# Layer 0's gate and up products as three products of rounded parts, with GpSimd making the rests

## The chip, the cores and the metric

The kernel runs on one core of one Trainium2 chip. The metric is the device time of one execution in microseconds (us). Five engines run their own instruction streams and meet only at semaphores: TensorE (PE; its weight loads are shown apart, as PEld), VectorE (DVE), ScalarE (ACT), GpSimd (POOL) and SyncE (SP, which here only issues transfers). Tiles have 128 partitions; matmul results land in 8 PSUM banks of 512 float32 columns.

## The reference, cut to what matters

Four layers of attention-like and feed-forward blocks run on 1024 tokens of width 256. Only layer 0 matters here. After a layer norm (`xn`) it adds two branches to `x`: a chunked linear attention, and a gated feed-forward whose weights are splines of a few control points.

```
xn = _layernorm(x)
# attention: q, k, v = xn @ w.T in 16 heads; q and k are each a product of two small linear maps
kv = cumsum over chunks of (kc^T vc), shifted by one chunk
o  = qc @ kv + mask(qc @ kc^T) @ vc         # then a norm per head, then o @ wo.T
# feed-forward, 1024 inner channels
gate = xn @ gate_w.T ; up = xn @ up_w.T
x = x + attention + (silu(gate) * up) @ down_w.T
```

A feed-forward of layer 3, far behind, uses weights rounded to three values per group of 64 ("ternary"). Their rounding doesn't depend on any layer, and the kernel does it early, beside layer 0.

## The kernel before

**Layer 0, projection stage.** `xT` holds the normalised input transposed: 2 halves (`k`) by 1024 tokens. ScalarE copies spline results into `V[0]` (gate), `V[1]` (up), `V[2]` (down), 2048 columns each, and VectorE overlays a second spline piece (`second_cubics`, L1274). TensorE projects q and k, then v (L483), then makes the two small linear maps of q and k (L537, 8 steps of two products). For each step ScalarE writes one factor (L974 or L976, into one of two buffers `f2s`) and VectorE multiplies it with the other (L1305). Ahead of its first L1305 VectorE works out the scales of the ternary groups: one long reduction (L1291) and four small tensor_scalar instructions (L1292 to L1295). Behind the last it writes `kpar`, k masked by head parity, in four tensor_scalar instructions of 1024 columns (L1311). TensorE's first score products (L555) wait for them.

**Layer 0, chunk loop.** Eight chunks `c` of 128 tokens. For each, TensorE runs in this order: the scores (L555), gate and up for the first 512 tokens (`gate_up0(c, 0, 0)` and `(c, 0, 1)`, L474), the new key-value product (L589), gate for the other 512 tokens, the product with the accumulated state (L597), the values (L573), and up for the other 512 tokens. In `gate_up0` the chunk number `c` picks 128 of the 1024 inner channels. VectorE masks the four score banks (L1334), multiplies silu(gate) with up (L1328, twice), masks and adds the state (L1341, L1344), and in chunks 0 to 5 does the first part of a ternary step. GpSimd does the rest of it:

```
if c < 6:
    if c:
        dve.wait_ge(tern_ready, c)
    dve.tensor_tensor(by_group(tern_t[0]), tern_part(c), tern_group(2, c), ALU.is_gt)
    dve.tensor_tensor(by_group(tern_t[1]), tern_part(c), tern_group(3, c), ALU.is_lt).then_inc(tern_signs, 1)
```

These are L1349 and L1350. GpSimd waits for `tern_signs`, runs four instructions on 1024 bf16 columns (L1737 to L1740) and increments `tern_ready`. VectorE's next step waits for that. GpSimd also copies v by head parity (`by_parity`, L1729), for `values0`.

**Behind the loop.** TensorE sums squares per head (L604), multiplies the hidden activations with the down weights (L483, 128 instructions), and then with `wo`. VectorE takes four reciprocals (L1359) with a product each (L1360), adds the results to `x`, and normalises for layer 1. GpSimd raises the variances to the power -1/2 (L1714), two instructions per layer.

A product of two float32 operands is issued as two TensorE instructions. Layer 1 already uses `split_product`, in which each operand is a pair of fp32r parts (a rounded one and the rest) and three products are added: hi by hi, hi by rest, rest by hi (L493, L494, L495). There ScalarE makes the rounded part and GpSimd (or VectorE) subtracts.

A PSUM bank is handed on in a fixed rotation (`group`): a product waits until the reader of the bank's last user is done (`reuse`). SP issues all transfers in program order, `lB` (layer 2 and expert gate weights) among the first ones.

Of the kernel before, what the change touches and what calls it, by code (L numbers as in the profile page):

```python
# [80 lines left out]
D_END = D_COL + 6  # L81


def build(nc, dram, out):

    ctx = ExitStack()
    with ctx:
        def sb(name, cols, dt=F32, parts=P):
            return ctx.enter_context(nc.sbuf_tensor(name, [parts, cols], dt))
# [5 lines left out]
        x = sb("x", NT * D)[:, :].rearrange("p (t d) -> p t d", t=NT)  # L95
        xT = sb("xT", KD * T)[:, :].rearrange("p (k t) -> p k t", k=KD)
        const = sb("const", C_COS)[:, :]
        rows = sb("rows", R_END, parts=1)[:, :]
        lB = sb("lB", B_END)[:, :]
# [11 lines left out]
        with nc.sbuf_tensor("arena0", [P, ARENA0], F32) as arena0:  # L111
            pass
        arena = sb("arena", ARENA)
# [109 lines left out]
        eprod_ready, ehid_hi = sem("eprod_ready"), sem("ehid_hi")  # L223
        out_done = sem("out_done")
# [3 lines left out]
        lA = m.cols(A_END + A_END % 2)  # L228
        hid0_at = m.at
        win, phase = m.cols(SPB), m.cols(SPB)  # L230
        hid0 = Carve(arena0, hid0_at).grid(NI, T)
        m.at = hid0_at + NI * T
# [5 lines left out]
        silu0 = Carve(arena0, f2s_at).grid(2, BW)  # L238
        V = [m.cols(SPB) for _ in range(3)]
# [156 lines left out]

        block = ctx.enter_context(nc.Block())
# [3 lines left out]
        def _(sp):  # L401
# [7 lines left out]
            sp.dma_start(lB, dram["lB"]).then_inc(lB_loaded, 16)  # L409
            sp.dma_start(lD, dram["lD"]).then_inc(lD_loaded, 16)  # L410

            sp.wait_ge(x_added, HEAD0["added"])
# [40 lines left out]
        def _(pe):  # L453
# [106 lines left out]
            def gate_up0(c, b, n):  # L560
                wide(g_gu0[c][b][n], lambda k: V[n][:, k * I0 + c * P:k * I0 + (c + 1) * P], xT, b)

# [16 lines left out]
            for c in range(NT):  # L579
                scores0(c)  # L580
                if c == 0:
                    pe.wait_ge(*g_spl[-1][-1][1].ready)
# [18 lines left out]
            for p, g in enumerate(g_sum0):  # L601
                reuse(g)
                pe.wait_ge(osq_ready, 2 * p + 2)
                pe.matmul(g.ps, bdmask, kvbd[:, 2 * p:2 * p + 2, :], start=True, stop=True).then_inc(g.full_sem, 1)  # L604
            pe.wait_ge(*g_gu0[NT - 1][NB - 1][1].ready)
# [318 lines left out]
        def _(act):  # L924
# [304 lines left out]
        def _(dve):  # L1229
# [99 lines left out]

            for c in range(NT):  # L1330
# [25 lines left out]
            for p, g in enumerate(g_sum0):  # L1356
# [350 lines left out]
        def _(pool):  # L1707
# [22 lines left out]

            by_parity(0)
            by_parity(1)
            for n in range(6):
                by_parity(n + 2)
# [6 lines left out]
                pool.wait_ge(tern_ready, n + 1)  # L1741

# [209 lines left out]
```

## Time and profile before

| what | value |
|---|---|
| three timed runs | 795.55 us median (792.79 to 795.62) |
| the profiled execution | 796.97 us, span 795.2 us |
| TensorE busy | 709.8 us (89%) |
| VectorE busy | 561.6 us (71%) |
| ScalarE busy | 370.7 us (47%) |
| GpSimd busy | 347.1 us (44%) |
| mean granted TensorE clock | 0.965 |

A share of the whole span is a mean over stages. The change touches the stretch from 56 to about 191 us, which is layer 0 from the q and k maps to the end of the down product, so that stretch is to be read by itself.

### The profile page before, as it was taken

Reading aid. Unit: us, or ns where it says so; the run is one execution under the profiler, and the core shown is the slowest. Engines: PE = TensorE matmul, PEld = TensorE weight load, DVE = VectorE, ACT = ScalarE, POOL = GpSimd, SP = SyncE. Lnnn points to the kernel's source line nnn. Section 1 sums busy time; section 2 is a strip of 40 time slices with the busy share of each in tenths; the row PEclk is TensorE's granted clock in tenths of the full one; section 3 lists DMA queues with packets and bytes.
Section 4 is the critical chain, followed back from the end, with each engine's and each line's share of the span. In section 5 each row is a group of like instructions: output and inputs, shape, how many; then the busy total and the mean of one; then the engine's idle time right before and its main releaser. Section 6 shows DMA issues by size and latency. Waiting matters only on the chain.

```text
span 795.2 us, 12530 instructions
## 1 busy us (share of the span) xinstructions
PE 709.8 (89%) x4172; PEld 550.7 (69%) x4172; DVE 561.6 (71%) x1096; ACT 370.7 (47%) x782; POOL 347.1 (44%) x260
## 2 busy tenths in 40 slices
PE   3899999998899999999999999998998898865567
PEld 1454555587488989898989899987987346554446
DVE  4256666584599797979797757564776455499995
ACT  2275111201465656565555656564554522575440
POOL 0100589300657474747474848441230110437651
PEclk9999999999999999999999999999999899978798
DMA  9400000000401010100101010001110000100001
GB/s 306 201 1 2 1 1 2 1 1 2 151 21 34 8 39 5 28 25 20 33 20 33 20 33 20 21 7 41 40 40 0 1 0 1 33 1 0 0 1 53
DMA packets 11328, 24.76 MB, mean 31 GB/s; under 512 B 1217, under 2 KB 5538, under 8 KB 10786
## 3 DMA queue, kind: packets, MB, share of 16 engines
q1 hardware_dynamic: 10928, 23.19, 8.8%
q10 hardware_dynamic: 370, 1.18, 0.5%
q8 instruction: 18, 0.29, 0.2%
q14 instruction: 12, 0.10, 0.0%
HBM read 23.31 MB, written 1.05 MB: 31 GB/s over the span
## 4 chain that ended last, share of the span: by engine, by line
PE 58%; DVE 24%; issue 7%; POOL 6%; ACT 3%; DMA 2%; DVEq 1%; SPq 0%; POOLq 0%; ACTq 0%
PE bank L493 9%; PE bank L495 8%; PE bank L494 8%; PE bank L483 7%; PE bank L474 7%; PE bank L659 4%; PE bank L689 3%; PE bank L688 2%; DVE x L1426 2%; PE bank L673 2%; DVE zone L1603 2%; PE bank L537 2%; DVE arena L1400 2%; DVE arena L1401 2%; DVE arena L1410 2%
## 5 line engine op out<-in xcount | busy, mean ns | idle before, releaser
L493 PE MATMUL bank<-zone 128*128 128x256 f32 (+1 forms) x520 | 180.5, 347 | 9.0 <-DVE arena L1401 4.0
L495 PE MATMUL bank<-zone 128*128 128x256 f32 (+1 forms) x520 | 169.9, 327 | 0.0
L494 PE MATMUL bank<-zone 128*128 128x256 f32 (+1 forms) x520 | 169.6, 326 | 0.0
L1751 POOL TENSOR_TENSOR arena<-arena 128x512 f32<-128x512 f32 x64 | 82.1, 1282 | 84.5 <-ACT arena L1044 75.7
L493 PEld LDWEIGHTS bank<-zone 128*128 128x128 f32 x520 | 99.4, 191 | 26.2 <-DVE arena L1401 9.5
L495 PEld LDWEIGHTS bank<-zone 128*128 128x128 f32 x520 | 99.3, 191 | 8.7
L494 PEld LDWEIGHTS bank<-zone 128*128 128x128 f32 x520 | 99.7, 192 | 6.6
L1756 POOL TENSOR_TENSOR arena<-arena 128x512 f32<-128x512 f32 x64 | 82.4, 1287 | 32.3 <-DVE arena L1401 23.0
L1745 POOL TENSOR_TENSOR zone<-arena,zone 128x512 fp32r<-128x512 f32 (+1 forms) x56 | 58.6, 1058 | 60.6 <-ACT zone L1106 47.7
L474 PE MATMUL bank<-xT,arena 128*128 128x512 f32 x160 | 77.2, 621 | 2.0 <-ACT xT L935 0.8
L1063 ACT ACTIVATE arena<-arena 128x256 f32<-128x256 f32 (+1 forms) x128 | 62.1, 487 | 32.0 <-DVE arena L1410 31.9
L1426 DVE SCALAR_TENSOR_TENSOR x<-bank,arena,x 128x256 f32<-128x256 f32 x128 | 53.0, 471 | 15.0 <-PE bank L495 14.7
L1410 DVE CUSTOM_DVE_ANT_0 arena<-bank,const 128x256 f32<-128x256 f32 (+1 forms) x128 | 46.2, 403 | 24.6 <-PE bank L659 24.4
L1714 POOL TENSOR_TENSOR lnw<-lnw,minus_half 128x4 f32<-128x4 f32 x8 | 8.1, 1015 | 125.1 <-DVE lnw L1248 125.1
L879 PE MATMUL bank<-zone 128*128 128x512 f32 x128 | 38.3, 455 | 25.4 <-DVE arena L1613 22.5
L659 PE MATMUL bank<-arena 128*128 128x256 f32 (+1 forms) x256 | 59.8, 366 | 0.0
L1400 DVE TENSOR_TENSOR arena<-bank,arena 64x512 f32<-64x512 f32 x64 | 44.4, 693 | 16.2 <-ACT arena L1044 14.7
L474 PEld LDWEIGHTS bank<-xT,arena 128*128 128x128 f32 x160 | 29.3, 195 | 33.4 <-issue 30.4
L879 PEld LDWEIGHTS bank<-zone 128*128 128x128 f32 x128 | 27.8, 225 | 34.8 <-DVE arena L1613 24.6
L689 PE MATMUL bank<-arena 128*128 128x128 f32 x256 | 49.5, 275 | 0.7 <-ACT arena L1031 0.7
L1044 ACT ACTIVATE arena<-bank 128x512 f32<-128x512 f32 x64 | 37.5, 586 | 24.6 <-PE bank L495 24.6
L659 PEld LDWEIGHTS bank<-arena 128*128 128x128 f32 x256 | 43.5, 190 | 4.5
(266 smaller groups left out, 1407.0 us busy)
## 6 DMA issues: line engine op xcount, KB each, us to landing
arena<-in_qk SPq DMA_DIRECT2D x16, 256.0 KB, 2.8
arena<-in_tern SPq DMA_DIRECT2D x1, 3072.0 KB, 22.0
arena<-in_wv SPq DMA_DIRECT2D x8, 256.0 KB, 2.8
arena<-in_wo SPq DMA_DIRECT2D x16, 128.0 KB, 2.1
arena<-in_w SPq DMA_DIRECT2D x8, 256.0 KB, 2.7
lB<-in_lB SPq DMA_DIRECT2D x1, 1288.5 KB, 24.5
arena<-in_lA SPq DMA_DIRECT2D x1, 1282.5 KB, 15.3
x<-in_x SPq DMA_DIRECT2D x1, 1024.0 KB, 12.9
```

The lines of the kernel that those rows point to most:

```text
L474: last = pe.matmul(g.ps, weight(k), act[:, k, b * BW:(b + 1) * BW], start=(k == 0), stop=(k == KD - 1))
L493: pe.matmul(dst, lhi, rhi, start=(n == 0), stop=False)
L494: pe.matmul(dst, lhi, rlo, start=False, stop=False)
L495: last = pe.matmul(dst, llo, rhi, start=False, stop=(n == len(terms) - 1 and not open_end))
L659: last = pe.matmul(ps[2 + g % 2][:, tt * 2 * P + lo:(tt + 1) * 2 * P], qT1[:, tok(t)], kT1[:, t * P - P + lo:t * P + P], start=True, stop= ...
L689: last = pe.matmul(ps[6 + g // 2][:, tok(t % TPB)], v1[:, t, mine], pT1[:, t, 1, :], start=(t == 0), stop=True)
L879: last = pe.matmul(g.ps, weight, part[:, k, b * BW:(b + 1) * BW], start=(k == 0 and m == 0), stop=(k == KD - 1 and m == 1))
L1063: last = act.activation(S1[:, t, lo:], S1[:, t, lo:], ACT.Exp, scale=-1.0, bias=nmax[:, t:t + 1], accum_out=rsum[:, t:t + 1])
L1410: last = dve.tensor_tensor_reduce(S1[:, t, lo:], ps[2 + g % 2][:, tt * 2 * P + lo:(tt + 1) * 2 * P], winmask[:, lo:], -SC1, 3.0e38, ALU.ad ...
L1426: last = dve.scalar_tensor_tensor(out=x[:, t, :], in0=ps[bank][:, tt * D:(tt + 1) * D], scalar=rinv[:, t:t + 1], in1=x[:, t, :], op0=ALU.m ...
L1751: pool.tensor_tensor(qraw[:, j, :], qraw[:, j, :], cosT[:, at], ALU.mult).then_inc(cos_done, 1)
L1756: pool.tensor_tensor((kT1, qT1)[j % 2][:, at], qraw[:, j, :], qsin[:, j, :], ALU.add).then_inc(qk_ready, 1)
```

## The change

Gate and up of layer 0 become `split_product`s. For that each operand gets two fp32r parts.

- `xT`: ScalarE writes rounded copies (four instructions of 512 columns) into memory in which `lB` lies otherwise. GpSimd subtracts them from `xT` and writes the rests over `xT` in place (four instructions).
- Weights: ScalarE writes rounded copies of `V[0]` and `V[1]` (`round_gu`, eight instructions of 512 columns) into `gu_part`, one ahead of each step's `f2s` instruction. GpSimd writes the rests over `V[0]` and `V[1]` (`rest_of_gu`, eight instructions), four of them ahead of the first two `by_parity` copies and four behind.
- TensorE waits for `xT0_split` and `gu_split` ahead of chunk 0 and for the last rests ahead of chunk 4.
- The ternary steps go to chunks 0, 2, 4 and 6, and the last two into VectorE's loop over the norm, behind its second and fourth pass.
- The load of `lB` moves behind the last gate and up product; `lD` moves up one place.

```diff
             def gate_up0(c, b, n):
-                wide(g_gu0[c][b][n], lambda k: V[n][:, k * I0 + c * P:k * I0 + (c + 1) * P], xT, b)
+                g, at = g_gu0[c][b][n], slice(b * BW, (b + 1) * BW)
+                reuse(g)
+                split_product(g.ps, [(parts([gu_part[:, c, (n * KD + k) * P:(n * KD + k + 1) * P], Vr[n][:, k * I0 + c * P:k * I0 + (c + 1) * P]]),
+                                      cut(parts(xT0), ALL, k, at)) for k in range(KD)]).then_inc(g.full_sem, 1)
...
                 if c == 0:
-                    pe.wait_ge(*g_spl[-1][-1][1].ready)
+                    pe.wait_ge(xT0_split, KD * NB)
+                if c % 4 == 0:
+                    pe.wait_ge(gu_split, 4 + c)
...
+            for k in range(KD):
+                for b in range(NB):
+                    at = slice(b * BW, (b + 1) * BW)
+                    act.activation(xT0[0][:, k, at].bitcast(F32R), xT[:, k, at], ACT.Copy).then_inc(xT0_hi, 1)
+
+            def round_gu(cc, n):
+
+                k, h = divmod(cc, 2)
+                act.wait_ge(*g_spl[cc][n][1].ready)
+                act.activation(gu_part[:, 4 * h:4 * h + 4, (n * KD + k) * P:(n * KD + k + 1) * P].bitcast(F32R),
+                               V[n][:, cc * BW:(cc + 1) * BW].rearrange("p (c i) -> p c i", c=4), ACT.Copy).then_inc(gu_hi, 1)
+
             for mm in range(4):
                 for b in range(NB):
                     n = mm * NB + b
+                    round_gu(GU_ORDER[n // 2], n % 2)
...
-                if c < 6:
-                    if c:
-                        dve.wait_ge(tern_ready, c)
-                    dve.tensor_tensor(by_group(tern_t[0]), tern_part(c), tern_group(2, c), ALU.is_gt)
-                    dve.tensor_tensor(by_group(tern_t[1]), tern_part(c), tern_group(3, c), ALU.is_lt).then_inc(tern_signs, 1)
+                if c % 2 == 0:
+                    ternary_signs(c // 2)
...
+                if p % 2:
+                    ternary_signs(4 + p // 2)
...
+            pool.wait_ge(*g_v0[-1].full)
+            for n in range(KD * NB):
+                k, b = divmod(n, NB)
+                at = slice(b * BW, (b + 1) * BW)
+                pool.wait_ge(xT0_hi, n + 1)
+                pool.tensor_tensor(xT0[1][:, k, at].bitcast(F32R), xT[:, k, at], xT0[0][:, k, at], ALU.subtract).then_inc(xT0_split, 1)
+            for n in range(4):
+                rest_of_gu(n)
             by_parity(0)
             by_parity(1)
+            for n in range(4, 8):
+                rest_of_gu(n)
             for n in range(6):
-                by_parity(n + 2)
+                if n < 3:
+                    by_parity(2 * n + 2)
...
+                if n < 3:
+                    by_parity(2 * n + 3)
...
             sp.dma_start(raw3, dram["tern"]).then_inc(raw_loaded, 16)
+            sp.dma_start(lD, dram["lD"]).then_inc(lD_loaded, 16)
+
+            sp.wait_ge(*g_gu0[NT - 1][NB - 1][1].full)
             sp.dma_start(lB, dram["lB"]).then_inc(lB_loaded, 16)
-            sp.dma_start(lD, dram["lD"]).then_inc(lD_loaded, 16)
```

## Rows read from the trace of the kernel before

**Rows 1.** Engines' busy time by stretch: us, PE, PEld, DVE, ACT, POOL, PEclk, DMA share, GB/s.

```profile
84.00:94.50 10.50, 10.50 (x104) 5.91 (x96) 7.40 (x12) 1.86 (x4) 7.87 (x4) 1.00 0.01 2
```

**Rows 2.** PE in order of time, chunk loop: start us, us, instructions, [idle before <-releaser].

```profile
83.20 1.17 PE L555 MATMUL bank<-arena 32*128 32x128 f32 x32
...
88.29 1.88 PE L474 MATMUL bank<-xT,arena 128*128 128x512 f32 x4
90.01 0.61 PE L597 MATMUL bank<-arena 128*128 128x128 f32 x4
...
93.48 1.17 PE L555 MATMUL bank<-arena 32*128 32x128 f32 x32
...
146.14 1.17 PE L555 MATMUL bank<-arena 32*128 32x128 f32 x32
```

**Rows 3.** The chain that ended last, one ternary step: start us, us, what.

```profile
105.28 1.23 DVE arena L1349
...
116.06 1.23 DVE arena L1349
```

**Rows 4.** PE in order of time, experts of layer 1, fp32r products of 512 columns.

```profile
546.05 0.39 PE L493 MATMUL bank<-zone 128*128 128x512 f32 x1
...
553.76 0.39 PE L494 MATMUL bank<-zone 128*128 128x512 f32 x1
```

**Rows 5.** DVE in order of time, beside an idle and beside a busy POOL.

```profile
79.27 0.43 DVE L1344 TENSOR_TENSOR arena<-arena 128x256 f32<-128x256 f32 x1
...
89.63 1.11 DVE L1344 TENSOR_TENSOR arena<-arena 128x256 f32<-128x256 f32 x1
...
691.85 3.00 DVE L1627 TENSOR_SCALAR arena<-arena,small 128x1024 f32<-128x1024 f32 x1 [8.29 <-ACT arena L1164]
694.88 4.31 DVE L1628 TENSOR_TENSOR_SCAN arena<-arena 128x1024 f32<-128x1024 f32 x1
699.12 0.66 DVE L1619 TENSOR_SCALAR arena<-arena 128x1024 f32<-128x1024 f32 x1
```

**Rows 6.** POOL in order of time, at the moment of the DVE row at 691.85.

```profile
691.89 5.16 POOL L1812 TENSOR_TENSOR arena<-arena 128x1024 f32<-128x1024 f32 x2 [6.06 <-ACT arena L1164]
```

**Rows 7.** All engines in order of time, projection stage.

```profile
55.76 13.91 PE L537 MATMUL bank<-arena 128*128 128x512 f32 x32
...
55.96 0.60 ACT L964 ACTIVATE arena<-bank 128x512 f32<-128x512 f32 x1 [1.13 <-PE bank L483]
...
59.44 0.21 DVE L1292 TENSOR_SCALAR tern_s<-tern_s 128x96 bf16<-128x96 f32 x1
...
60.48 1.41 DVE L1305 SCALAR_TENSOR_TENSOR arena<-bank,arena 128x512 f32<-128x512 f32 x2 [0.22 <-DVE tern_s L1295]
...
70.49 2.74 DVE L1311 TENSOR_SCALAR arena<-arena,const 128x1024 f32<-128x1024 f32 x4
...
73.37 1.17 PE L555 MATMUL bank<-arena 32*128 32x128 f32 x32 [0.90 <-DVE arena L1311]
```

**Rows 8.** Groups by line and shape, 0 to 260 us: busy us, mean ns, idle before.

```profile
L1745 POOL TENSOR_TENSOR zone<-arena,zone 128x512 fp32r<-128x512 f32 x6 | 7.8, 1306 | 5.4 <-DMA arena<-in_cossin 5.3
L1334 DVE TENSOR_TENSOR arena<-bank,const 128x512 f32<-128x512 f32 x32 | 19.8, 679 | 1.0 <-PE bank L555 1.0
L1050 ACT ACTIVATE zone<-arena 128x512 fp32r<-128x512 f32 x4 | 2.5, 634 | 1.6 <-DMA arena<-in_qk 1.6
```

**Rows 9.** Behind the loop: PE, DVE and POOL in order of time.

```profile
155.87 3.60 PE L604 MATMUL bank<-arena,const 128*128 128x512 f32 x8
...
171.15 3.35 DVE L1359 RECIPROCAL arena<-arena 128x512 f32<-128x512 f32 x1
...
193.01 1.02 POOL L1714 TENSOR_TENSOR lnw<-lnw,minus_half 128x4 f32<-128x4 f32 x1 [44.63 <-DVE lnw L1248]
```

**Rows 10.** Transfers by tile: issues, KB each, median us to landing.

```profile
arena<-in_lA SPq DMA_DIRECT2D x1, 1282.5 KB, 15.3
```

**Rows 11.** Engines' busy time by stretch, columns as in the first group.

```profile
542.00:544.00 2.00, 2.00 (x5) 1.61 (x6) 0.00 (x0) 0.00 (x0) 0.04 (x1) 0.50 0.76 220
```

More of the change, by code:

```diff
@@ L81 @@
 D_END = D_COL + 6
+LA_COLS = -(-A_END // 16) * 16
+GU_HI = LA_COLS + (NI // 2) * T
+GU_LO = LA_COLS + NI * T + 2 * P + SPB // 2
 def build(nc, dram, out):
@@ L95, in build @@
         x = sb("x", NT * D)[:, :].rearrange("p (t d) -> p t d", t=NT)
+        with nc.sbuf_tensor("rounded_x", [P, 2 * KD * T], F32) as rounded_x:
+            rounded_x = rounded_x[:, :]
         xT = sb("xT", KD * T)[:, :].rearrange("p (k t) -> p k t", k=KD)
+        lB = sb("lB", B_END)[:, :]
         const = sb("const", C_COS)[:, :]
         rows = sb("rows", R_END, parts=1)[:, :]
-        lB = sb("lB", B_END)[:, :]
         lD = sb("lD", D_END)[:, :]
@@ L112, in build @@
             pass
+        with nc.sbuf_tensor("below_hi", [P, GU_HI], F32):
+            with nc.sbuf_tensor("gu_hi0", [P, NI * 4 * P], F32) as gu_hi0:
+                pass
+        with nc.sbuf_tensor("below_lo", [P, GU_LO], F32):
+            with nc.sbuf_tensor("gu_lo0", [P, 2 * SPB], F32) as gu_lo0:
+                pass
         arena = sb("arena", ARENA)
@@ L223, in build @@
         eprod_ready, ehid_hi = sem("eprod_ready"), sem("ehid_hi")
+        xT0_hi, xT0_split, gu_hi, gu_split = sem("xT0_hi"), sem("xT0_split"), sem("gu_hi"), sem("gu_split")
         out_done = sem("out_done")
         m = Carve(arena0)
-        lA = m.cols(A_END + A_END % 2)
+        lA = m.cols(LA_COLS)
         hid0_at = m.at
@@ L231, in build @@
         hid0 = Carve(arena0, hid0_at).grid(NI, T)
+        gu_part = Carve(gu_hi0).grid(NI, 4 * P)
+        xT0 = [rounded_x.rearrange("p (a k t) -> p a k t", a=2, k=KD)[:, 1 - a] for a in range(2)]
         m.at = hid0_at + NI * T
@@ L238, in build @@
         silu0 = Carve(arena0, f2s_at).grid(2, BW)
+        assert m.at == GU_LO and hid0_at + (NI // 2) * T == GU_HI
+        Vr = [Carve(gu_lo0, n * SPB).cols(SPB) for n in range(2)]
         V = [m.cols(SPB) for _ in range(3)]
@@ L395, in build @@
         g_down3 = [group(x_added, b) for b in SUMS]
+        GU_ORDER = (0, 2, 1, 3)
         block = ctx.enter_context(nc.Block())
@@ L604, in _ @@
                 pe.matmul(g.ps, bdmask, kvbd[:, 2 * p:2 * p + 2, :], start=True, stop=True).then_inc(g.full_sem, 1)
+            pe.wait_ge(*g_spl[-1][-1][1].ready)
             pe.wait_ge(*g_gu0[NT - 1][NB - 1][1].ready)
@@ L1328, in hidden0, with ternary_signs @@
                 dve.tensor_tensor(hid0[:, c, b * BW:(b + 1) * BW], g.ps, silu0[:, (c * NB + b) % 2, :], ALU.mult).then_inc(g.ready_sem, 1)
+            def ternary_signs(n):
+                if n:
+                    dve.wait_ge(tern_ready, n)
+                dve.tensor_tensor(by_group(tern_t[0]), tern_part(n), tern_group(2, n), ALU.is_gt)
+                dve.tensor_tensor(by_group(tern_t[1]), tern_part(n), tern_group(3, n), ALU.is_lt).then_inc(tern_signs, 1)
             for c in range(NT):
@@ L1729, in by_parity, with rest_of_gu @@
                 pool.tensor_copy(own, v0[:, c, :].rearrange("p (g r e) -> p r g e", r=2, e=DK0)).then_inc(vpar_ready, 1)
+            def rest_of_gu(at_n):
+                cc, n = GU_ORDER[at_n // 2], at_n % 2
+                k, h = divmod(cc, 2)
+                pool.wait_ge(gu_hi, at_n + 1)
+                whole = V[n][:, cc * BW:(cc + 1) * BW].rearrange("p (c i) -> p c i", c=4)
+                rest = Vr[n][:, cc * BW:(cc + 1) * BW].rearrange("p (c i) -> p c i", c=4)
+                pool.tensor_tensor(rest.bitcast(F32R), whole, gu_part[:, 4 * h:4 * h + 4, (n * KD + k) * P:(n * KD + k + 1) * P],
+                                   ALU.subtract).then_inc(gu_split, 1)
+            pool.wait_ge(*g_v0[-1].full)
[6 more added lines that the diff above has]
+                rest_of_gu(n)
             by_parity(0)
             by_parity(1)
+            for n in range(4, 8):
+                rest_of_gu(n)
             for n in range(6):
-                by_parity(n + 2)
+                if n < 3:
+                    by_parity(2 * n + 2)
                 w, (t0, t1) = tern_part(n), [by_group(t) for t in tern_t]
```

## The prediction

> **What bounds the kernel now.** I read the page first: TensorE is busy 89% of the span and carries 58% of the chain that ended last. Then the stretches, to see whether that holds where the change sits. In the chunk loop TensorE is busy 10.50 of 10.50 us at a granted clock of 1.00, VectorE 7.40, GpSimd 7.87 [rows 1]. Then TensorE in order of time. The scores of one chunk start at 83.20 and of the next at 93.48, so an unhindered chunk takes 10.28 us. From 83.20 to 146.14 there are six chunks, 62.94 us, where six of 10.28 would be 61.68. So 1.26 us of the loop is waiting [rows 2]. The chain shows for what: a ternary step goes round VectorE and GpSimd in 10.78 us (105.28 to 116.06), a little slower than TensorE's 10.28 [rows 3]. So two limits lie close together in the loop, TensorE's work first and the ternary round second, and the change loosens both. The reader should not take the chain's many GpSimd pieces there as the price of the ternary steps: removing them alone is worth 1.3 us.
>
> **TensorE's gain.** Gate and up take 16 instructions per chunk, at one start every 0.43 us: four of them fill 88.29 to 90.01, which is 1.72 us [rows 2]. That is 6.88 us. After it they are 2 (gate, up) by 2 (halves of the tokens) by 2 (`k`) by 3 products, 24 instructions. The same helper with the same shape starts 34 instructions in the 7.71 us from 546.05 to 553.76, one every 0.227 us [rows 4]: 24 take 5.44 us. The difference is 1.44 us per chunk, 11.5 us for eight. The bounds: the 24 can't be faster than these rows, and at the worst the switches between float32 and fp32r products cost 0.1 us each, four a chunk, which leaves 8.3 us. I take 11.5, since nothing but the order of neighbours differs.
>
> **The ternary round.** One step per two chunks, so one round of 10.78 us against two chunks of 10.28 - 1.44 = 8.84 us each. The 1.3 us of waiting go. Sum of gains: 12.8 us.
>
> In a chunk that follows a ternary step VectorE starts the score masks later. Counted from that chunk's first score product: product for L1328 ends 0.8, two comparisons of 1.23 us end 3.3, four masks of about 0.6 end 3.9 to 5.8 [rows 3, 8]. TensorE needs the first mask's bank for the third gate/up group, at 1.1 (scores) + 2.7 + 0.5 = 4.3 us, and the fourth mask at about 6.2, for the values. Both are in time by 0.4 us. If VectorE were late by more, it would delay four chunks by the excess.
>
> **What ScalarE adds.** Twelve copies of 512 columns, 0.63 us each [rows 8]. Four come behind its v copy of 55.96, so they end near 58.7 [rows 7]. The eight others go one to a step, and a step takes TensorE 13.91 / 8 = 1.74 us while ScalarE then needs 0.63 + 0.65. It catches up. Cover: TensorE's own 13.9 us. Without that cover 7.6 us would show. I take nothing.
>
> **What GpSimd adds, and whom it blocks.** Twelve subtractions of 512 columns at 1.31 us [rows 8], 15.7 us in all, from about 57.2 on, in a stretch where GpSimd did next to nothing before. They are needed by chunk 0 (eight of them, ready near 68 to 69) and chunk 4, so by themselves they delay nobody. But they meet VectorE. At 691.85 VectorE's tensor_scalar on SBUF and a pair of GpSimd subtractions start together; the tensor_scalar takes 3.00 us where the same form takes 0.66 at 699.12, and the next VectorE instruction takes 4.31 us [rows 5, 6]. Read as turns: one GpSimd instruction, one of VectorE, the second of GpSimd, the second of VectorE. The addition with both inputs in SBUF does the same on a smaller scale: 0.43 us beside an idle GpSimd, 1.11 us beside a ternary step [rows 5]. The masks with one input in PSUM hold 0.68 us in the mean over all 32, most of them beside a busy GpSimd [rows 8], so such instructions don't wait.
>
> In the projection stage two groups of VectorE are of the first kind. (a) The four small L1292 to L1295, at 59.44 [rows 7]: each waits up to one subtraction of 1.31 us. Three are chained, so GpSimd takes its turn between them. That puts L1295's end near 64.3 where the first L1305 began at 60.48, about 3.8 us late. TensorE can be four steps ahead; its second product of step 4 wants its bank at about 63.6 and gets it at 65.2. From there on ScalarE and VectorE pace the stage: ScalarE needs about 1.2 us a step with its new copy, and the last L1305 ends about 2.3 us later than before. (b) `kpar`, four instructions in 2.74 us at 70.49 [rows 7]. By then GpSimd has one or two subtractions left, shifted by the same turns: each costs one turn, 1.4 us in total by my placing of them. TensorE waits for `kpar` directly (L555 at 73.37 is idle before it until L1311) [rows 7]. Together 3.7 us. The low end is 0.5 us (the small ones don't queue, GpSimd is through before 70.5); the high end is eight turns less the 2.5 us that (a) has in hand, 8 x 1.31 - 2.5 = 8.0 us. I take 3.7, since the row at 691.85 shows turns and the slack is read from rows.
>
> The Trainium skill ("SBUF — State Buffer", section "Who interferes with whom") says that a VectorE instruction in a two-port mode, tensor_scalar among the candidates, and a GpSimd instruction exclude each other for the whole of an instruction, and that one with at most one SBUF input outside these modes never meets GpSimd. The row at 691.85 agrees with the exclusion. The Trainium skill's page also says that whoever starts first goes first, where the row shows VectorE started 0.04 us earlier and still lost the turn; by the order of the Trainium skill's page the sum would change by less than one turn, 1.3 us. By the same page of the Trainium skill the L1305 and the reduction L1291 stay as they are; no row here shows the reduction beside GpSimd.
>
> **What is moved.** `lB`'s load is issued at the end of the loop and needed 40 us later, behind down, `wo` and the norm; `lA`, as large, landed in 15.3 us behind other loads [rows 10]. SP's next wait is behind down and `wo` as well, so nothing queued behind it starts later. Cost nothing; it would cost one for one past 40 us. `lD` has no waiting reader in either place. The `by_parity` copies: `by_parity` 3, 5 and 7 now follow a ternary step that ends at least a chunk before the values need them. No cost.
>
> Behind the loop VectorE gets two more pairs of comparisons. Counted from the loop's end (155.87 before): norm passes 0 and 1 end at 11, comparisons at 14, passes 2 and 3 at 22 to 24 (their second instructions have two SBUF inputs and may wait one turn each), comparisons at 27, against the last reciprocal's end at 18.6 before [rows 9]. The fourth down product comes at about 31, so the adds are in time by some 3 us. GpSimd's last step ends near 34, and the power for the norm came 37.1 us behind the loop's end [rows 9]. It is free by about 3 us. No cost, but the cover is thin.
>
> **Sum.** 12.8 - 3.7 = 9.1 us. The profiled execution took 796.97 us (span 795.2), so 787.9 in its terms. It is 1.4 us above the median of the runs shown, 795.55, which gives 786.5 us.
>
> **The rivals.**
> Forecast: both gains come, VectorE and GpSimd take turns as above, 784.5 to 789. Chance 0.55.
> Rival 1, no turns in the projection stage: the small instructions don't queue and GpSimd is through by `kpar`. Loss 0.5 us, time 783.3, 782.5 to 784.5. For it: GpSimd's position at 70.5 is my placing. Against it: the row at 691.85. Chance 0.18.
> Rival 2, more of it: TensorE idles for several microseconds ahead of chunk 0 and its clock falls. At 542 to 544 the granted clock was 0.50 after a thin stretch [rows 11]; some 4 us at that level cost 2 us. Or the turns reach 8.0 us. Or a late mask costs some tenths in four chunks. 788.5 to 791.5. Chance 0.15.
> Rival 3, the tail: the last ternary step holds GpSimd when the norm of layer 1 wants it. 3 us of slack, then one for one. If the two norm passes and the step itself lose 8 us instead of the 3 I counted, the time is 791.5: no measurable change. Chance 0.06.
> Rival 4, slower: every VectorE instruction of the projection stage waits for GpSimd, L1305 too. Then all of GpSimd's new work, 15.7 us and two copies of 0.4, lies on the path, less the slack of 2.5: 14.0 us against 12.8, time 796.8. It is slower by over 0.5% from a delay of 16.8 us on, so turns that also stretch GpSimd's own instructions by a fifth decide it, at 799.6. Against it: the masks' 0.68 us. Chance 0.06.
>
> Rival 1 and the forecast hold 0.73, rival 2 brings it to 0.88. The range goes from 783 to 791. About 0.5%, 4 us, is what a measurement of this kernel can tell from no change: faster means below 791.6, slower above 799.5. Chances: faster 0.85, within 0.10, slower 0.05.
>
> **What would show it.** Starts of two neighbouring score groups 8.8 to 8.9 us apart. L493 to L495 in the loop one start every 0.227 us, no idle before them by L1334. L1292 to L1295 spread over more than 3 us; L1311 lasting 4 us or more; the first scores of the loop at 77 instead of 73.4; then the loop's end near 147. L1714 of layer 1 with idle time before it, released by VectorE. The prediction is wrong if the chunks take 9.3 us or more (a VectorE wait), if the first scores come past 82, or if L1714 waits for GpSimd's own L1740.

## The result, and the profile after

| | before | after |
|---|---|---|
| median of five runs each | 795.62 us (792.79 to 796.63) | 787.28 us (786.71 to 788.79) |
| profiled execution | 796.97 us, span 795.2 | 786.71 us, span 784.9 |
| ratio of the times, 95% interval | | 0.9902 (0.9881 to 0.9923) |

Faster by 8.3 us in the medians, 10.3 us between the two profiled executions. The forecast was a gain of 9.1 us to 786.5 us, range 783 to 791. The total came out; two of its three terms were too large and their errors largely cancelled. So the parts are the interesting thing. Line numbers moved with the edit: each new number is named beside its old one where it matters.

The stretch of the chunk loop that [rows 1] showed before, and the whole of the unhindered loop, by engine (columns as in [rows 1]):

```profile
84.00:94.50 10.50, 10.50 (x131) 8.47 (x124) 8.53 (x13) 1.85 (x4) 7.49 (x4) 1.00 0.01 2
76.00:146.00 70.00, 70.00 (x740) 55.74 (x733) 46.00 (x69) 17.50 (x35) 32.75 (x21) 1.00 0.01 1
```

TensorE is busy in all 70.00 us at a granted clock of 1.00. Nothing else holds the loop any more: VectorE has 24 us to spare and GpSimd 37. The same stretch in order of time, TensorE (L574 was L555, the scores; L512 to L514 are the three products of rounded parts; L628 was L604, down):

```profile
55.52 7.89 PE L556 MATMUL bank<-arena 128*128 128x512 f32 x18
64.10 6.28 PE L556 MATMUL bank<-arena 128*128 128x512 f32 x14 [0.69 <-DVE arena L1343]
...
75.09 1.17 PE L574 MATMUL bank<-arena 32*128 32x128 f32 x32 [1.90 <-DVE arena L1349]
...
83.63 1.17 PE L574 MATMUL bank<-arena 32*128 32x128 f32 x32
...
91.03 0.50 PE L512 MATMUL bank<-rounded_x,gu_hi 128*128 128x512 f32 x1
91.37 0.39 PE L513 MATMUL bank<-rounded_x,gu_hi 128*128 128x512 f32 x1
...
137.55 1.17 PE L574 MATMUL bank<-arena 32*128 32x128 f32 x32
...
146.00 3.59 PE L628 MATMUL bank<-arena,const 128*128 128x512 f32 x8
```

Three readings. The loop, from the first scores to down, takes 146.00 - 75.09 = 70.91 us, where before it took 82.50 (73.37 to 155.87) [rows 7, 9]: 11.59 us gained, 12.8 forecast. From 83.63 to 137.55 six chunks take 8.99 us each, with no idle time shown; 8.84 was forecast. Within a run the products start every 0.233 us, but the first of a run costs 0.34 (91.03 to 91.37). And the first scores start 19.57 us behind the first product of the q and k maps (L556, was L537); before it was 73.37 - 55.76 = 17.61 [rows 7]. So the start of the loop lost 1.96 us, where 3.7 was forecast. 11.59 - 1.96, and 0.24 us by which the projection stage happened to start earlier, are the 9.87 us between 155.87 and 146.00.

VectorE in the projection stage (L1330 to L1333 were L1292 to L1295, L1343 was L1305, L1349 was L1311):

```profile
59.21 0.38 DVE L1330 TENSOR_SCALAR tern_s<-tern_s 128x96 bf16<-128x96 f32 x1
59.62 1.20 DVE L1331 TENSOR_SCALAR tern_s<-tern_s 128x96 f32<-128x96 bf16 x1
60.85 1.19 DVE L1332 TENSOR_SCALAR tern_s<-tern_s 128x96 f32<-128x96 f32 x1
61.96 1.30 DVE L1333 TENSOR_SCALAR tern_s<-tern_s 128x96 f32<-128x96 f32 x1
63.30 1.41 DVE L1343 SCALAR_TENSOR_TENSOR arena<-bank,arena 128x512 f32<-128x512 f32 x2
...
70.42 0.75 DVE L1343 SCALAR_TENSOR_TENSOR arena<-bank,arena 128x512 f32<-128x512 f32 x1 [0.34 <-PE bank L556]
71.21 3.83 DVE L1349 TENSOR_SCALAR arena<-arena,const 128x1024 f32<-128x1024 f32 x4
```

GpSimd in the same stretch (L1790 makes the rests of `xn`, L1782 those of the weights):

```profile
57.01 4.97 POOL L1790 TENSOR_TENSOR rounded_x<-xT,rounded_x 128x512 fp32r<-128x512 f32 x4 [30.66 <-ACT rounded_x L994]
61.92 4.96 POOL L1782 TENSOR_TENSOR gu_lo<-arena,gu_hi 128x512 fp32r<-128x512 f32 x4
...
67.52 4.98 POOL L1782 TENSOR_TENSOR gu_lo<-arena,gu_hi 128x512 fp32r<-128x512 f32 x4
```

The turns are in plain sight: instructions of 0.21 us take 1.20, close to GpSimd's step of 4.96 / 4 = 1.24 us. L1343, which reads one input from PSUM, keeps its 0.75 us in the same company. `kpar` (L1349) takes 3.83 us instead of 2.74 [rows 7]: 1.1 us, for the one subtraction left at 71.2 to 72.5.

Behind the loop, GpSimd (L1758 was L1714, the norm's power; L1805 was L1740, the last operation of a ternary step):

```profile
177.91 2.13 POOL L1805 TENSOR_TENSOR w<-w,arena 128x1024 bf16<-128x1024 bf16 x1
183.02 1.02 POOL L1758 TENSOR_TENSOR lnw<-lnw,minus_half 128x4 f32<-128x4 f32 x1 [2.98 <-DVE lnw L1286]
```

The power starts at 183.02, released by VectorE, after 2.98 us of idle time: the tail's slack, forecast as 3 us. Before it started at 193.01 [rows 9], so 9.99 us of the gain reach layer 1. From there on the same instructions of the two traces stay 10.2 to 10.3 us apart to the end.

Of the signs that the prediction named, the late start by way of L1330 to L1333 (4.05 us from 59.21 to 63.26, over 3 us forecast) and the power released by VectorE are there. The others are there in a smaller size: `kpar` took 3.83 us and not 4 or more, the first scores came at 75.09 and not 77, the chunks are 8.99 us apart and not 8.8 to 8.9, the products 0.233 us and not 0.227.

### The profile page after: what moved, and what is told of

It is laid out like the page before. It is cut to its first block, busy times and chain, and to the rows that moved or that the text cites. A ratio compares the mean times of both kernels' runs of the same rounds, so it can differ in the third digit from the quotient of the medians.

```text
span 784.9 us, 12684 instructions
## 1 busy us (share of the span) xinstructions
PE 698.7 (89%) x4236; PEld 562.2 (72%) x4236; DVE 564.3 (72%) x1096; ACT 376.5 (48%) x794; POOL 359.4 (46%) x272
## 4 chain that ended last, share of the span: by engine, by line
PE 64%; DVE 23%; issue 7%; ACT 3%; POOL 1%; DMA 1%; DVEq 1%; SPq 0%; POOLq 0%; ACTq 0%
PE bank L512 11%; PE bank L514 10%; PE bank L513 10%; PE bank L502 6%; PE bank L493 5%; PE bank L684 4%; PE bank L714 3%; PE bank L713 2%; DVE x L1470 2%; PE bank L698 2%; DVE zone L1647 2%; DVE arena L1454 2%; DVE arena L1444 2%; DVE arena L1445 2%; DVE arena L1431 2%
## 5 line engine op out<-in xcount | busy, mean ns | idle before, releaser
L512 PE MATMUL bank<-zone 128*128 128x256 f32 (+1 forms) x520 | 180.4, 347 | 9.0 <-DVE arena L1445 3.9
L514 PE MATMUL bank<-zone 128*128 128x256 f32 (+1 forms) x520 | 169.9, 327 | 0.0
L512 PEld LDWEIGHTS bank<-zone 128*128 128x128 f32 x520 | 99.4, 191 | 25.9 <-DVE arena L1445 9.4
L514 PEld LDWEIGHTS bank<-zone 128*128 128x128 f32 x520 | 99.3, 191 | 8.7
L1444 DVE TENSOR_TENSOR arena<-bank,arena 64x512 f32<-64x512 f32 x64 | 44.3, 693 | 16.0 <-ACT arena L1082 14.5
L714 PE MATMUL bank<-arena 128*128 128x128 f32 x256 | 49.5, 275 | 0.7 <-ACT arena L1069 0.7
L1758 POOL TENSOR_TENSOR lnw<-lnw,minus_half 128x4 f32<-128x4 f32 x8 | 8.1, 1016 | 83.1 <-DVE lnw L1286 83.1
L713 PE MATMUL bank<-arena 128*128 128x128 f32 x224 | 44.9, 282 | 0.0
L1445 DVE TENSOR_TENSOR arena<-bank,arena 64x512 f32<-64x512 f32 x64 | 43.7, 684 | 0.8
```

The costliest lines, as they stand in the source:

```text
L512: pe.matmul(dst, lhi, rhi, start=(n == 0), stop=False)
L514: last = pe.matmul(dst, llo, rhi, start=False, stop=(n == len(terms) - 1 and not open_end))
L713: pe.matmul(ps[6 + g // 2][:, tok(t % TPB)], v1[:, t - 1, mine], pT1[:, t, 0, :], start=True, stop=False)
L714: last = pe.matmul(ps[6 + g // 2][:, tok(t % TPB)], v1[:, t, mine], pT1[:, t, 1, :], start=(t == 0), stop=True)
```

## The experiments

**1. No turns.** GpSimd's first rests wait until VectorE's four short instructions are through, its last four until `kpar` is made.

```diff
@@ GpSimd, ahead of the rests @@
             pool.wait_ge(*g_v0[-1].full)
+            pool.wait_ge(tern_sum, 1)
             for n in range(KD * NB):
...
             by_parity(0)
             by_parity(1)
+            pool.wait_ge(kpar_ready, 2 * KD)
             for n in range(4, 8):
                 rest_of_gu(n)
```

> The changed kernel with two waits more on GpSimd: its first subtraction waits until VectorE's four small scale instructions are through, and its last four subtractions wait until kpar is written. Nothing of the computation is changed. My theory (VectorE's tensor_scalars on SBUF and GpSimd's subtractions take turns, and this alone holds the loop's start back by 1.7 us): the small ones take 0.2 us each again, kpar 2.7 to 3.0 us, the first scores of the loop come at 73.4 to 73.7 instead of 75.1, and the time is 1.4 to 1.7 us below the changed kernel's 787.3. Rival (the late start comes from ScalarE's twelve copies, which pace the q and k maps): the start stays at 75 and the time at 787.3.

Measured: 785.8 us (781.24 to 786.47), ratio to before 0.9859 (0.9833 to 0.9885). VectorE and TensorE of this kernel:

```profile
59.26 0.20 DVE L1333 TENSOR_SCALAR tern_s<-tern_s 128x96 f32<-128x96 f32 x1
...
71.36 2.74 DVE L1349 TENSOR_SCALAR arena<-arena,const 128x1024 f32<-128x1024 f32 x4
```

```profile
56.64 13.90 PE L556 MATMUL bank<-arena 128*128 128x512 f32 x32
...
74.24 1.17 PE L574 MATMUL bank<-arena 32*128 32x128 f32 x32 [0.89 <-DVE arena L1349]
```

The short ones are back at 0.20 us, `kpar` at 2.74, the maps run unbroken, and the scores start 17.60 us behind them, as before the change. ScalarE's twelve copies are still in this kernel, so the whole delay of the start is the turns.

Layer 1 takes part of it back for a time. Around its first product:

```profile
195.09 2.65 POOL L1814 TENSOR_TENSOR zone<-arena,zone 128x512 fp32r<-128x512 f32 x2 [6.01 <-DMA arena<-in_cossin]
```

```profile
196.51 0.47 PE L512 MATMUL bank<-zone 128*128 128x512 f32 x1 [1.59 <-POOL zone L1814]
```

GpSimd waits there for a transfer of layer 1, and TensorE for GpSimd; the changed kernel's TensorE has no idle time at that place. Counted from the maps' first product, VectorE's instructions at 200 us stand 1.0 us earlier than in the changed kernel, where the norm's power stood 2.0 us earlier. At the end of the trace it is 2.0 us again; why, no run shows.

**2. Only the short ones spared.** The first of the two waits alone. GpSimd's last four rests then fall on `kpar`.

> The changed kernel with the first of the two waits alone. GpSimd begins at 60.1 instead of 57.0, so it is still at its last four subtractions when kpar is written. Turns: kpar's four instructions meet about four subtractions of 1.24 us, take about 6.7 us instead of 3.8, and the scores start near 77.3, 2.2 us later than in the changed kernel, time about 789.5. Rival (VectorE is served first or isn't held): kpar takes 2.7 us, start 73.4, time 785.6.

Measured: 788.75 us (787.71 to 790.4), ratio 0.9916 (0.9895 to 0.9937).

```profile
70.88 6.16 DVE L1349 TENSOR_SCALAR arena<-arena,const 128x1024 f32<-128x1024 f32 x4
```

```profile
71.42 6.74 POOL L1782 TENSOR_TENSOR gu_lo<-arena,gu_hi 128x512 fp32r<-128x512 f32 x4
```

```profile
77.09 1.17 PE L574 MATMUL bank<-arena 32*128 32x128 f32 x32 [4.23 <-DVE arena L1349]
```

Both engines are stretched: 2.74 to 6.16 us on VectorE, 4.98 to 6.74 on GpSimd, and the 7.28 us from 70.88 to 78.16 that they take together are close to the sum of what each needs alone, 2.74 + 4.98 = 7.72 us. The scores start 20.93 us behind the maps, 3.3 more than without turns. Then the granted clock falls as well:

```profile
78.00:80.00 2.00, 2.00 (x16) 1.56 (x9) 1.90 (x4) 1.76 (x3) 0.16 (x1) 0.54 0.03 8
```

Chunk 0 takes 10.06 us (77.09 to 87.15) instead of 8.54, so 1.5 us of this kernel's time are the clock's and not the turns'.

**3. The products alone.** The changed kernel with a ternary step in every chunk, as before.

```diff
@@ VectorE, chunk loop @@
-                if c % 2 == 0:
-                    ternary_signs(c // 2)
+                if c < 6:
+                    ternary_signs(c)
@@ VectorE, behind the norm's pass p @@
-                if p % 2:
-                    ternary_signs(4 + p // 2)
@@ GpSimd, ternary step n @@
-                if n < 3:
-                    by_parity(2 * n + 2)
+                by_parity(n + 2)
...
                 pool.wait_ge(tern_ready, n + 1)
-                if n < 3:
-                    by_parity(2 * n + 3)
```

> The changed kernel with the ternary steps back in chunks 0 to 5. My theory: the round of a ternary step through VectorE and GpSimd, 10.78 us, now sets the pace of chunks 1 to 6, so the loop ends near 154.3, only some 1.6 us earlier than before the change, and the time is about 794; TensorE waits about 1.8 us a chunk for the masks. Rival (the ternary step isn't on the path, as TensorE's own work bounded the loop before): only the 1.3 us that the moved steps gave are missing, time 788.6.

Measured: 799.42 us (796.94 to 799.67), ratio 1.0041 (1.0021 to 1.0062). The direction was right, since the products are worth little while the ternary round binds, but it is slower than before by 3 to 4 us where about 794 had been expected. GpSimd, about one round:

```profile
101.97 2.14 POOL L1799 TENSOR_TENSOR arena<-arena 128x1024 bf16<-128x1024 bf16 x1 [1.16 <-DVE arena L1373]
...
106.17 2.19 POOL L1801 TENSOR_TENSOR arena<-arena,w 128x1024 bf16<-128x1024 bf16 x1
108.44 2.15 POOL L1802 TENSOR_TENSOR w<-w,arena 128x1024 bf16<-128x1024 bf16 x1
...
113.27 2.14 POOL L1799 TENSOR_TENSOR arena<-arena 128x1024 bf16<-128x1024 bf16 x1 [1.16 <-DVE arena L1373]
```

Stretches of the same kernel, columns as in [rows 1]:

```profile
76.00:82.00 6.00, 5.92 (x41) 4.92 (x42) 3.00 (x12) 3.66 (x5) 0.00 (x0) 0.50 0.01 3
...
136.00:142.00 6.00, 5.54 (x46) 4.46 (x47) 4.25 (x7) 1.26 (x3) 5.84 (x3) 0.72 0.01 3
```

A round takes 11.30 us (101.97 to 113.27), not the 10.78 of [rows 3]: the step's last two operations take 2.19 and 2.15 us, where the kernel before has 1.95 and 1.89. And the granted clock is at 0.50, the lower of its two levels (1.2 GHz), from 76 to 82, and mixed from 136 to 142, both behind waits of TensorE: chunk 0 takes 11.43 us, the chunk from 129.78 to 142.64 takes 12.86. The chunk before that had a wait of the same length:

```profile
125.15 0.50 PE L512 MATMUL bank<-rounded_x,gu_hi 128*128 128x512 f32 x1 [2.05 <-DVE arena L1379]
...
136.46 0.50 PE L512 MATMUL bank<-rounded_x,gu_hi 128*128 128x512 f32 x1 [2.05 <-DVE arena L1379]
```

Behind the first of these two waits the granted clock stayed at 1.00 (11.30 us for the chunk), behind the second it fell. So the length of the wait doesn't settle it.

In this execution the maps run unbroken from 56.50. `kpar` starts 14.72 us behind their start, as before the change (70.49 - 55.76 = 14.73), and only its own turns make it late:

```profile
71.22 4.80 DVE L1349 TENSOR_SCALAR arena<-arena,const 128x1024 f32<-128x1024 f32 x4
```

The start comes 19.58 us behind the maps (76.08), as in the changed kernel, whose code up to there is the same.

**4. The ternary steps alone.** The kernel before with comparisons in every other chunk and two steps behind the norm's passes: the same edits as in experiment 3, in the other direction.

> The kernel before with the ternary steps moved as in the change, products and loads as they were. My theory: chunks of 10.28 us throughout, the loop ends 1.3 us earlier, at 154.6, time 794.3. Rival (moving the steps is worth more, as the chain of waits showed 15% of the span on GpSimd's four ternary instructions): 785 to 790.

Measured: 793.87 us (791.76 to 795.17), ratio 0.9976 (0.9955 to 0.9997).

```profile
134.83 1.17 PE L555 MATMUL bank<-arena 32*128 32x128 f32 x32
145.10 1.17 PE L555 MATMUL bank<-arena 32*128 32x128 f32 x32
...
154.84 1.45 PE L604 MATMUL bank<-arena,const 128*128 128x512 f32 x3
```

The second to the seventh chunk take 10.27 us each, and the loop 154.84 - 73.63 = 81.21 us instead of 82.50: 1.29 us, forecast 1.26 to 1.3. The two edits are worth 1.29 us (ternary alone) and 11.59 together, so the products are worth 10.3 us, but only with the ternary steps out of the way.

**5. `lB`'s load late, alone.** The kernel before, with the load behind the last gate and up product.

```diff
-            sp.dma_start(lB, dram["lB"]).then_inc(lB_loaded, 16)
             sp.dma_start(lD, dram["lD"]).then_inc(lD_loaded, 16)
+
+            sp.wait_ge(*g_gu0[NT - 1][NB - 1][1].full)
+            sp.dma_start(lB, dram["lB"]).then_inc(lB_loaded, 16)
```

> The kernel before with one edit, the move of lB's load behind the last gate and up product (lD's goes up). My step gave the move nothing: the load is over long before the norm and the router want it. So 795.4, a ratio within 0.3% of 1, and the same slack before the last recipients of lB. A rival, in which the transfer now meets other loads of layer 1: 797 or more, with a wait on the queue in front of the router's first product.

Measured: 795.86 us (794.2 to 798.24), ratio 1.0001 (0.9983 to 1.0018). Its issue and landing:

```profile
lB<-in_lB SPq DMA_DIRECT2D x1, 1288.5 KB, 5.9
```

The load lands in 5.9 us, and its first reader comes at 197.8, 42 us behind the issue at 155.9. The move costs nothing, as forecast.

**6. Everything from the arena on, 8 columns further.** One unused tile ahead of it in the changed kernel.

```diff
+        sb("shift", 8)
         with nc.sbuf_tensor("arena0", [P, ARENA0], F32) as arena0:
```

> The changed kernel with everything from the arena on 8 columns (32 bytes) further on, so that the rounded weights and their rests begin on another boundary. In the changed kernel the rounded products of gate and up came every 0.233 us, those of the experts every 0.227. If placement makes the difference, the loop's products fall to 0.227 here, a chunk gets some 0.15 us shorter (24 of them) and the time about 1 us less, 786.2. If the loop's surroundings do (changes of form, accumulation groups of twelve), 0.233 and 787.3 stay. GpSimd's two last operations of a ternary step, 2.20 and 2.14 us in the changed kernel, show by the same token whether they go by the place of their work area.

Measured: 786.84 us (784.46 to 789.3), ratio 0.9884 (0.9845 to 0.9924): not told apart from the changed kernel's time. In the trace there is a small effect:

```profile
76.33 2.09 PE L575 MATMUL bank<-arena 32*128 32x128 f32 x32 [2.63 <-DVE arena L1350]
86.42 1.17 PE L575 MATMUL bank<-arena 32*128 32x128 f32 x32
95.34 1.17 PE L575 MATMUL bank<-arena 32*128 32x128 f32 x32
```

A chunk takes 8.93 us, not 8.99; inside a run the products start every 0.2305 us (mean of 128 pairs), where the changed kernel has 0.2333 (128 pairs) and the experts of layer 1 0.2273 in either. So placement makes 0.06 us a chunk, half a microsecond in all, and half of the step from 0.227 to 0.233. Chunk 0 shows something else: 10.09 us, its first group 2.09 instead of 1.17, behind 2.63 us of idle time. The granted clock is at 0.72 in the mean from 76 to 82. The shift need not be the cause, since experiments 2 and 3 show the same without it.

**7. Both last ternary steps behind the last norm pass.**

```diff
-                if p % 2:
-                    ternary_signs(4 + p // 2)
+                if p == NT // 2 - 1:
+                    ternary_signs(4)
+                    ternary_signs(5)
```

> The changed kernel with both of the last ternary steps behind the third and last of the norm's passes instead of one behind the second. My step gave the tail 3 us of slack: GpSimd was free at 180.0 and wanted at 183.0. Here step 4 starts some 12 us later than in the changed kernel and steps 4 and 5 take two rounds of 11.3 us, so GpSimd is free about 190 to 192, 7 to 9 us after it is wanted, and VectorE's adds of the residual come late too: 794 to 796. If the tail has more cover than I think (something else sets the norm's power), the time stays at 787.3.

Measured: 789.22 us (786.38 to 795.2), ratio 0.9932 (0.9901 to 0.9963). GpSimd:

```profile
185.70 2.12 POOL L1806 TENSOR_TENSOR w<-w,arena 128x1024 bf16<-128x1024 bf16 x1
187.90 1.02 POOL L1759 TENSOR_TENSOR lnw<-lnw,minus_half 128x4 f32<-128x4 f32 x1
```

The power now has no idle time before it: GpSimd is what it waits for, and VectorE's input to it was ready 2.2 us earlier (L1286 ends at 185.65). It comes 4.88 us later than in the changed kernel (183.02), of which 0.45 us is a later start of the maps in this execution, and layer 1's products come 4.8 us later (201.82 for 197.03). GpSimd is free 7.3 us later by the same count; less the slack of 2.98 that leaves 4.4, and 4.4 us it is. So the cover of the tail is real and thin, and past it a delay passes on one for one. I had expected GpSimd free at 190 to 192; it was free at 187.8, because without a ternary step among them VectorE's norm passes end at 165.8 and the comparisons start at once. The median moved by 1.9 us only. In this profiled execution the same VectorE instructions stay 4.72 us behind those of the changed kernel from 210 to 535 us, and are 1.75 behind at the end. The traces of experiments 2 and 3, in which nothing is changed there either, come nearer to the changed kernel's by 2.6 and 2.4 us between 540 and 690, so that part is not the edit's. What the later part does to the median, over runs spread across 9 us, I leave open.

**8. Experiment 3 with the ternary work area 6 columns further.** `tern_t` stands 10 float32 columns from its old place in the changed kernel, since `lA` was rounded up from 2566 columns to 2576; here it stands 16.

```diff
+        m.cols(6)
         tern_t = [m.cols(512).bitcast(BF16) for _ in range(2)]
```

> The run with the products alone (ternary steps one a chunk, as in the kernel before; 799.4 us) with the ternary work area 6 columns further on, so that it stands 16 columns (64 bytes) from its place in the kernel before, not 10. If GpSimd's longer operations there (2.19 and 2.15 us in place of 1.95 and 1.89) come from that placement, they are back at 1.95 and 1.89, the round from 11.3 to 10.8, and five rounds take 2.6 us less: 796.8. If they come from something else, such as more traffic of TensorE's reads, 799.4 stays.

Measured: 795.92 us (791.32 to 799.51), ratio 1.0013 (0.999 to 1.0036).

```profile
113.22 1.95 POOL L1802 TENSOR_TENSOR arena<-arena,w 128x1024 bf16<-128x1024 bf16 x1
115.25 1.89 POOL L1803 TENSOR_TENSOR w<-w,arena 128x1024 bf16<-128x1024 bf16 x1
```

The operations are back at 1.95 and 1.89 us, and the scores come 10.8 us apart (114.23, 125.03, 135.83). The longer operations came from the place of the tile. Experiment 3's profiled execution spent 5.4 us more in the loop (84.74 against 79.34), 2.9 us of it in chunk 0 and 2.1 in the chunk at 129.78, mostly for the clock, which is at 1.00 in the same stretches here. The clock is not shown to go by the place of the tile. With both gone the loop takes 79.34 us (75.73 to 155.07), 3.2 less than before: its first chunks, ahead of the ternary steps, are short, the others go by the round of 10.8 us. The turns at the start cost 2 of the 3.2, and the median shows nothing of the rest.

**9 to 11. On one chip: the changed kernel again, no turns again, and all three edits** (no turns, 8 columns, and `tern_t` at 32 columns from its old place).

> The changed kernel once more, so that the next two runs are compared with it on one chip: 787.3.

> The first experiment's kernel again (GpSimd's rests wait until VectorE's short operations are done), beside the changed kernel on one chip. Its scores started 1.97 us sooner after the maps' first product than the changed kernel's, yet at layer 1's first products its profile stood only 0.9 us better by that measure of the same start, since the loads of layer 1 came last there. If the start is what it gains, 785.4 to 786.4; if layer 1's loads swallow it, 787.3.

> The same waits, the arena 8 columns further on (products at 0.231 instead of 0.233 in the run that did this alone, a chunk of 8.93 instead of 8.99 us, 0.5 us over the loop), and the ternary work area 14 columns further in it, at 32 columns from its place in the kernel before, so that GpSimd's operations on it take 1.95 and 1.89 us again. GpSimd is early in this arrangement of steps, so the last brings nothing but a freer tail. By the sum: 0.5 us under the run without turns, 785 to 786; if placement gains nothing together with the waits, the same as that run.

| | median | ratio to before, 95% |
|---|---|---|
| changed kernel | 787.15 us (786.88 to 789.43) | 0.9891 (0.9871 to 0.9911) |
| no turns | 784.04 us (782.32 to 786.43) | 0.9844 (0.9819 to 0.9868) |
| all three | 783.64 us (781.08 to 786.04) | 0.9839 (0.9813 to 0.9864) |

The start of the loop in the changed kernel, run again:

```profile
75.79 1.17 PE L574 MATMUL bank<-arena 32*128 32x128 f32 x32 [1.92 <-DVE arena L1349]
```

and with no turns:

```profile
74.43 1.18 PE L574 MATMUL bank<-arena 32*128 32x128 f32 x32 [0.89 <-DVE arena L1349]
```

The maps began at 56.21 and 56.83, so the scores follow them by 19.58 and 17.60 us: 1.98 us, as in the first pair. The medians differ by 3.1 us, more than that, and the median without turns lies below both of the times expected for it, 785.4 to 786.4 and 787.3; the rest lies within the spread of either kernel (2.6 and 4.1 us) and I can't assign it. Placement on top of it, 0.4 us in the median, can't be told from nothing, though the chunks are 8.93 us apart (91.74 to 136.37 in five) and GpSimd's operations 1.96 and 1.89 us. In that run the scores start 17.92 us behind the maps, since two `by_parity` copies of GpSimd fell on `kpar` (3.14 us instead of 2.74): the waits spare it the subtractions and not these. The version without turns beats both kernels.

## Why the prediction came out, term by term

**TensorE's gain: 11.5 forecast, 10.3 measured.** Right in kind, 1.2 us too large in size. I took the experts' 0.227 us [rows 4] for all 24 products. They run at 0.233 within a run, and at the changes to and from the float32 products some starts lie 0.08 to 0.11 us further apart, 0.37 us a chunk: 5.97 us for 24 products, where I had 5.44. The 16 float32 products had such steps too, 0.29 us a chunk, which my 6.88 left out:

```profile
84.31 3.70 PE L474 MATMUL bank<-xT,arena 128*128 128x512 f32 x8
87.84 0.61 PE L589 MATMUL bank<-arena 128*128 128x128 f32 x4
...
91.56 1.98 PE L474 MATMUL bank<-xT,arena 128*128 128x512 f32 x4
```

The three blocks before took 3.53 us (84.31 to 87.84), 1.72 and 1.92 (91.56 to 93.48), 7.17 in all. So the blocks got 1.20 us shorter, and the four starts of the new key-value product (L613, was L589), which I had not counted, 0.09 us; eight times 1.29 is 10.3. Most of what was missing is thus the slower step, 24 times 0.006 = 0.15 us a chunk. The changes between formats, which I had named as the bound at 0.4 us a chunk, cost 0.08 us more than the changes that were there before. Half of the slower step is placement (experiment 6); what makes the rest of the difference to the experts' 0.227 no run shows.

**The ternary round: 1.26 forecast, 1.29 measured** (experiment 4). The chain's view had shown GpSimd all over the loop, and the right price was still the waiting and not the time of the pieces. The waiting is in the last chunks alone:

```profile
114.03 1.17 PE L555 MATMUL bank<-arena 32*128 32x128 f32 x32
...
124.57 1.17 PE L555 MATMUL bank<-arena 32*128 32x128 f32 x32
...
135.36 1.17 PE L555 MATMUL bank<-arena 32*128 32x128 f32 x32
```

The three chunks up to 114.03 take 10.27 or 10.28 us, the next three 10.54, 10.79 and 10.78: the round falls behind by half a microsecond a chunk, and TensorE feels it only when its lead is used up. Experiments 3 and 8 show the other face of it: with faster products and the round left alone, the round binds and little of the gain is left.

**The turns: 3.7 forecast, 1.96 measured.** The mechanism was right, and experiments 1 and 2 show it from both sides. The sizes were not. All counts here are from the maps' first product, since it came 0.24 us earlier than before. Group (a) made the first L1343 3.1 us late instead of 3.8, since each turn cost a step of GpSimd's, 1.24 us, less the own time of what waited, and the first of the four slipped through in 0.38. From there ScalarE and VectorE caught up faster than I counted: a step of both took 1.10 us (66.03, 67.13, 68.23), not 1.2, so that the last L1343 was 1.0 us late, not 2.3. I had started from ScalarE's durations, 0.63 and 0.65, but its instructions start closer together than their durations add up to (64.73, 65.25, 65.82). Group (b) met one subtraction and cost 1.1 us, not 1.4.

The split between the two groups is not fixed, and their sum nearly is. In the changed kernel's execution VectorE's first short instruction starts 3.69 us behind the maps' first product; in experiment 3's it starts 2.00 us behind it, with the same code up to there. There group (a) delays nothing that shows, group (b) meets two subtractions and costs 2.06 us, and the scores are as late, 19.58 us behind the maps. In both `kpar` ends 2.5 us behind GpSimd's last subtraction (75.04 behind 72.50, 76.02 behind 73.49). So in these executions the delay went by when GpSimd was through, where I had added it up from the instructions that it blocks. Experiment 1 ran with the short offset too. That the turns of the short instructions break the maps is therefore shown by experiment 2, which had the long offset, no turns of theirs, and unbroken maps.

The Trainium skill ("SBUF — State Buffer", section "Who interferes with whom") has the two engines exclude each other for whole instructions when VectorE's is in a two-port mode, which a tensor_scalar on SBUF can be, and leaves alone an instruction with at most one input from SBUF and a reduction. Here the trace agrees: 0.21 became 1.20 us for L1331, L1343 kept 0.75 us beside the same subtractions, and the long reduction (L1329, was L1291) took 6.55 us as before, with subtractions beside its last 2 us. That page of the Trainium skill gives the turn to whoever issues first; the profile shows starts and not issues, so the row at 691.85 in the prediction doesn't contradict it.

**Nothing for the rest.** ScalarE's copies and `lB` cost nothing (experiment 1 for the former, 5 for the latter), the masks came in time (no idle time of TensorE in the loop), the tail's slack was 2.98 us for a forecast 3, and experiment 7 shows that it was cover and not an accident: used up, it turns into a delay of 4.4 us for the norm's power.

**The rivals.** Rival 1 (no turns) names about the time that experiments 1 and 9 to 11 reach by construction: 783.3 forecast, 785.8, 784.0 and 783.6 measured. Rival 2's mechanism, the clock that falls ahead of chunk 0, is nearer than its chance said. Behind 1.90 to 1.92 us of idle time (the changed kernel, its second run, experiments 7 and 8) the granted clock stayed at 1.00, its level of 2.4 GHz. Behind 2.63 us (experiment 6), 2.87 (experiment 3) and 4.23 (experiment 2) it fell, and chunk 0 took 10.09, 11.43 and 10.06 us instead of 8.54. Experiment 3 has the changed kernel's code up to the loop; its execution had the offset of 2.00 us named above, unbroken maps, and more of the idle time right ahead of the scores. So the changed kernel can meet this fall too; how often its timed runs do, no trace shows. Rival 4 is refuted by L1343's 0.75 us. Its second price has a slip: a fifth on GpSimd's 16.5 us is to be added before the slack of 2.5 is taken off, which gives 17.3 us and 800.0, not 799.6.

So the total was right because 11.59 for 12.8 lost 1.2 us and 1.96 for 3.7 gave 1.7 back: 9.6 us by the trace for a forecast 9.1. That the two errors nearly cancel is luck. Had only one of the two been mis-sized, the range of 783 to 791 would still have held it.

## What to carry to other kernels

Price an instruction in the surroundings in which it will run: the experts' rows gave 0.227 us a product where the loop gave 0.233, and starts at a change of form lay 0.1 us further apart, in the float32 products before as in their replacement. Where work goes to an engine that looks idle, list what its neighbour does in the same stretch with both operands in SBUF, and put a wait in front of the new work if it has time: two waits on GpSimd, whose results were needed later anyway, were worth 2 us at the start of the loop and 3 in the medians. And when two limits lie close together, one edit alone tells nothing about its worth: the products alone brought 3 us of the loop at best (experiment 8) and nothing of the time, with the ternary steps moved they brought 10.3 us.

## What the runs showed of the hardware that was not expected

GpSimd's operations on bfloat16 tiles of 128 x 1024 depend on where a tile stands. With `tern_t` at 0, 16 or 32 float32 columns from its old place, the step's last two operations, which also read or write the weights, take 1.95 and 1.89 us; with it at 10 or 18 columns they take about 2.2 and 2.15 in the loop. That is half a microsecond a step from rounding up an unrelated tile, hidden in the changed kernel and 0.5 us a chunk where the round binds. The clock is the other. It fell in three executions behind a wait ahead of the loop, and the chunk behind it took 1.5 us longer behind 2.63 us, 2.9 behind 2.87 and 1.5 behind 4.23; inside experiment 3's loop one wait of 2.05 us left it alone and the next of the same length did not. So a wait ahead of dense work can cost more than itself, and its length alone doesn't say how much.
